# Values product by one level of Strassen, in blocks of 256 queries, with x streamed from memory

## The chip, the cores and the metric

The kernel runs on one NeuronCore of a Trainium2 chip. The metric is the device time of one execution in microseconds (us). The engines are TensorE (PE in profile rows; PEld is its weight load), VectorE (DVE), ScalarE (ACT), GpSimd (POOL) and SyncE (SP), which here issues nearly all DMAs.

## The reference

x is 4096x512, adj is 4096x4096, both float32. Layer 0 is dense attention with adj added twice to the logits; layer 1 is a graph attention of 8 heads.

```python
q, k, v = x @ Wq.T + bq, x @ Wk.T + bk, x @ Wv.T + bv
attn = softmax(q @ k.T / sqrt(512) + adj + adj)
x = layernorm(x + attn @ v)
feats = einsum('nf,hfd->hnd', x, W)
dense = leaky_relu(e_self[:, :, None] + e_neigh[:, None, :]) + NEG_INF * (1.0 - adj)
out = relu(einsum('hnm,hmd->hnd', softmax(dense), feats) + b)
x = layernorm(x + out)
```

With adj up to 5.4 and NEG_INF = -1e10, the second softmax picks one neighbour per row: the one with the largest adj. The kernel finds that column, proves that the pick is safe, and gathers its row of feats; a general path for other inputs stands in the program and is not taken.

## The kernel before, in words

Every float32 matrix is split into two float16 parts, hi and lo, and a product is three matmuls (hi*hi, hi*lo, lo*hi) per 128x128 weight tile (`split_product`, L476). ScalarE makes the hi part, VectorE or GpSimd the lo part.

First stage, over 8 groups of 512 tokens: x is split into `xT`, which stays in SBUF; TensorE makes the values (4 tiles, PSUM banks S) and the transformed queries (4 tiles, banks O); both are split and stored to memory (`v_scratch`, `y_scratch`).

Main loop: 8 blocks of 512 queries by 32 key tiles of 128, 256 steps s. In step s TensorE makes the scores of chunk s: keys on partitions, 12 matmuls of 512 columns (L476, S). VectorE adds adj (`add`, L859) into a slot of `ring` and keeps a running maximum (`maximum`, L871). A block's softmax needs the maximum over all keys, so everything else follows 34 steps later (LAG). For chunk e = s-33 VectorE subtracts the broadcast maximum (`subtract`, L853), ScalarE takes exp into `pf` (L704) and makes the hi part (L653), GpSimd makes the lo part (L430) and adds to the row sums (`sacc`, L438). For chunk s-34 TensorE runs the values product: 4 banks O (128 queries each) by 3 matmuls of 512 columns (`values`, L533).

Once per block (`turn`) VectorE evicts the four banks (`evict`, L896); over the next steps each 128-row tile goes through statistics, normalisation (L912), its split (L768), 8 transposes (L572) and its feats product (12 matmuls, L476 X). Between them VectorE scans adj in 256 pieces of 128x512 with MAX8 (L829) and FIND_INDEX8 (L831). After the last values product come the last block's tiles, 32 indirect gathers of feats on GpSimd, the last layernorm and the output.

Order on each engine is program order; semaphores are counters on which an engine, or SP before a DMA, waits. The S banks alternate, so the scores of chunk c wait for `add` of c-2. The values product waits for the lo part.

## Time and profile before

| | |
|---|---|
| median of 3 runs | 1746.85 us (1746.17 to 1750.89) |
| profiled execution | 1754.84 us |
| its span, first to last instruction | 1753.1 us |
| mean granted TensorE clock | 0.971 |
| scores begin / first values product / last values product ends | 205.6 / 304.2 / 1652.7 us |
| TensorE busy, 490 to 1400 us | 908.75 of 910 us |
| VectorE, GpSimd busy there | 747.40 and 443.02 us |

An engine's busy time counts its instructions; a matmul's end is modelled and overlaps the next start, so for TensorE the spacing of starts is the better measure. "Idle before" is the time an engine sat waiting, with what released it.

### The profile page before, as it was taken

To read this page: it belongs to the slowest core of one execution; us is meant where nothing else is said; L and a number is where in the kernel's file an instruction comes from. 1 tells how busy PE (TensorE), PEld (TensorE's weight loads), DVE (VectorE), ACT (ScalarE), POOL (GpSimd) and SP (SyncE) were. 2 spreads that over 40 slices of the span, in tenths; PEclk is the share of its full clock that TensorE was granted. 3 is DMA by queue.
4 is the path that set the end of the run, shared out by engine and by line. 5 is a ranking of instruction groups with operands and counts; after the bars stand their busy time and mean duration, and the time that the engine had idled before them with its cause. 6 is when DMAs were issued, how large, how long until landed. Compare 5 with 4: busy or idle time off the path is not lost.

```text
span 1753.1 us, 22063 instructions
## 1 busy us (share of the span) xinstructions
PE 1641.7 (94%) x7748; PEld 750.8 (43%) x7748; DVE 1227.6 (70%) x2191; ACT 495.9 (28%) x765; POOL 736.6 (42%) x667
## 2 busy tenths in 40 slices
PE   8989999999999999999999999999999999999830
PEld 3334344444444444444444444444444444444310
DVE  4343255778897879778978797888887888754146
ACT  5334200222232223222222222222222222234327
POOL 2000000546444635464446444543455444568643
PEclk9999999999999999999999999999999999999965
DMA  6443434455555554555555455545555555446348
GB/s 216 145 162 120 166 110 127 151 187 162 180 163 200 172 175 162 181 191 165 166 197 181 162 187 181 186 160 182 168 199 164 173 163 191 139 126 210 109 132 294
DMA packets 150480, 298.25 MB, mean 170 GB/s; under 512 B 16352, under 2 KB 16352, under 8 KB 147424
## 3 DMA queue, kind: packets, MB, share of 16 engines
q1 hardware_dynamic: 147808, 288.42, 50.0%
q0 software_dynamic: 2560, 8.39, 1.5%
q8 instruction: 63, 1.03, 0.2%
q14 instruction: 49, 0.40, 0.1%
HBM read 253.76 MB, written 42.99 MB: 169 GB/s over the span
## 4 chain that ended last, share of the span: by engine, by line
PE 82%; DVE 7%; POOL 4%; ACT 3%; issue 2%; DMA 1%; ACTq 0%; DVEq 0%; SPq 0%; POOLq 0%
PE S L476 39%; PE O L533 32%; PE O L476 5%; PE X L476 4%; POOL ring L458 1%; POOL sacc L438 1%; POOL ring L430 1%; PE X L572 1%; DVE xT L768 1%; PE O L483 1%; DVE xr L896 1%; DVE ring L853 1%; DVE cidx L831 1%; DVE cand L829 1%; ACT xT L653 1%
## 5 line engine op out<-in xcount | busy, mean ns | idle before, releaser
L533 PE MATMUL O<-vring,ring 128*128 128x512 f16 x3072 | 704.6, 380 | 3.1 <-POOL ring L430 3.0
L476 PE MATMUL S<-yb,xT 128*128 128x512 f16 x3072 | 702.4, 380 | 4.2 <-DVE ring L859 4.2
L430 POOL TENSOR_TENSOR ring<-pf,ring 128x512 f16<-128x512 f32 x256 | 296.2, 1157 | 905.3 <-ACT ring L653 905.3
L476 PEld LDWEIGHTS S<-yb,xT 128*128 128x128 f16 x3072 | 301.2, 98 | 371.3 <-issue 7.6
L533 PEld LDWEIGHTS O<-vring,ring 128*128 128x128 f16 x3072 | 299.6, 98 | 358.0 <-issue 7.7
L704 ACT ACTIVATE pf<-ring 128x512 f32<-128x512 f32 x256 | 161.2, 630 | 995.5 <-DVE ring L853 970.0
L438 POOL TENSOR_TENSOR sacc<-sacc,pf 128x512 f32<-128x512 f32 x248 | 330.7, 1334 | 0.0
L859 DVE TENSOR_TENSOR ring<-S,ring 128x512 f32<-128x512 f32 x256 | 176.0, 687 | 176.5 <-PE S L476 169.4
L871 DVE TENSOR_TENSOR mx<-mx,ring 128x512 f32<-128x512 f32 x248 | 215.4, 868 | 8.5
L829 DVE MAX8 cand<-piece 128x8 f32<-128x512 f32 x256 | 175.0, 684 | 27.5 <-DMA piece<-in_adj 26.5
L853 DVE TENSOR_TENSOR ring<-BC,ring 128x512 f32<-128x512 f32 x256 | 172.4, 680 | 10.4 <-PE BC L559 10.4
L831 DVE FIND_INDEX8 cidx<-cand,piece 128x8 uint32<-128x512 f32 x256 | 175.4, 685 | 0.0
L653 ACT ACTIVATE ring<-pf 128x512 f16<-128x512 f32 x256 | 161.2, 630 | 8.1
L476 PE MATMUL S<-ring,xT 128*128 128x512 f16 x384 | 91.1, 398 | 12.3 <-DVE vring L768 12.3
L476 PE MATMUL X<-yb,x1T 128*128 128x512 f16 x384 | 93.5, 396 | 4.5 <-ACT x1T L653 4.5
L476 PE MATMUL O<-xT,ring 128*128 128x512 f16 x384 | 84.2, 379 | 0.0
L806 DVE TENSOR_TENSOR yb<-pf,yb 128x512 f16<-128x512 f32 x32 | 23.2, 725 | 61.8 <-ACT yb L688 61.8
L476 PEld LDWEIGHTS S<-ring,xT 128*128 128x128 f16 x384 | 38.4, 102 | 63.4 <-DVE vring L768 15.2
L476 PEld LDWEIGHTS X<-yb,x1T 128*128 128x128 f16 x384 | 38.5, 101 | 53.7 <-issue 7.2
L476 PEld LDWEIGHTS O<-xT,ring 128*128 128x128 f16 x384 | 37.6, 98 | 45.3
L768 DVE SCALAR_TENSOR_TENSOR vring<-S,vring 128x512 f16<-128x512 f32 x32 | 21.5, 688 | 49.9 <-ACT vring L653 49.9
L443 POOL TENSOR_TENSOR xr<-xr,bvb 128x512 f32<-128x512 f32 x32 | 45.6, 1424 | 0.0
(98 smaller groups left out, 696.8 us busy)
## 6 DMA issues: line engine op xcount, KB each, us to landing
ring<-in_adjT SPq DMA_DIRECT2D x256, 256.0 KB, 3.1
vring<-v_scratch SPq DMA_DIRECT2D x256, 256.0 KB, 2.7
piece<-in_adj SPq DMA_DIRECT2D x256, 256.0 KB, 3.7
ring<-in_xT SPq DMA_DIRECT2D x8, 1024.0 KB, 7.4
v_scratch<-vring SPq DMA_DIRECT2D x32, 256.0 KB, 2.1
y_scratch<-yb SPq DMA_DIRECT2D x8, 1024.0 KB, 4.9
yb<-y_scratch SPq DMA_DIRECT2D x8, 1024.0 KB, 6.7
xr<-in_x SPq DMA_DIRECT2D x32, 256.0 KB, 5.0
```

The lines of the kernel that those rows point to most:

```text
L430: pool.tensor_tensor(ring16[:, e % SLOTS, 1, :], pf[:, e % NPF, :], ring16[:, e % SLOTS, 0, :], ALU.subtract).then_inc(lo_done, 1)
L438: pool.tensor_tensor(sacc[:, :], sacc[:, :], pf[:, e % NPF, :], ALU.add).then_inc(sum_done, 1)
L443: pool.tensor_tensor(xr[:, j, :], xr[:, j, :], bvb[:, :], ALU.add).then_inc(xr_set, 1)
L476: mm = pe.matmul(psum, sta(a, k), mov(b, k), start=(k + a + b == 0), stop=(k == n - 1 and a == 1))
L533: mm = pe.matmul(O[j][:, :], ring16[:, e % SLOTS, a, j * P:(j + 1) * P], vring[:, e % NV, m, :], start=(k + a + m == 0), stop=(k == NT - 1 ...
L653: return nc.scalar.activation(dst, src, ACT.Copy, scale=scale)
L704: nc.scalar.activation(pf[:, e % NPF, :], ring[:, e % SLOTS, :], ACT.Exp, scale=-2.0).then_inc(exp_done, 1)
L829: dve.max(cand[:, q, :], part).then_inc(cand_set, 1)
L831: dve.max_index(cidx[:, q, :], cand[:, q, :], part).then_inc(cidx_set, 1)
L853: dve.tensor_tensor(slot, BC[:, :], slot, ALU.subtract).then_inc(sub_done, 1)
L859: dve.tensor_tensor(slot, S[c % 2][:, :], slot, ALU.add).then_inc(add_done, 1)
L871: dve.tensor_tensor(mx[:, :], mx[:, :], slot, ALU.max).then_inc(max_done, 1)
```

## The change

The values product of a step is now 256 queries (two tiles of 128) by 256 keys (two tiles) by 512 value columns (two halves), seen as a 2x2 by 2x2 product of 128x128 and 128x256 blocks, and done with 7 products instead of 8. Each is three matmuls of 256 columns, so a step has 21 of them where 12 of 512 columns (as much as 24 of 256) stood. The seven stationary operands are sums and differences of exp tiles, made in every step in `pfc`: the sums by GpSimd, the differences by VectorE (`exp_differences`). The seven moving operands are sums and differences of value tiles, made once in the first stage; six stay in SBUF (`vc`), the seventh is streamed (`vsum`). Banks O hold seven accumulators (`PRODUCTS`), and `combine` puts them together once per block, with three copies by ScalarE.

Blocks have 256 queries: 16 blocks of 16 steps, each step 256 keys; the lag is 19 steps. The scores of a step are 24 matmuls of 256 columns. SBUF no longer holds x: its split tiles are streamed through `xring`, five slots of 256 KB, two per chunk, and the weights of the feats product pass through the same slots. GpSimd no longer adds the bias of the values to x (it is in the values). At a turn the scores of two chunks run ahead of the first values product of the next block, and the next step has none. In the last 16 chunks VectorE makes the large lo part (`last_lo`, line 1087) instead of GpSimd. The scan does MAX8 alone; per row tile one piece is gathered again (GpSimd, indirect) and FIND_INDEX8 runs on it (`find`).

```diff
+    QB = 256
+    JB = QB // P
...
+    NP = NT // 2
+    NC = NB * NP
+    G = 512
+    GT = G // P
+    NG = N // G
+    LAG = NP + 3
+    AHEAD = 3
+    SLOTS = LAG + 2
+    NX = 5
+    NVS = 3
     PW = 512
     NPC = N // PW
     NSC = 3
-    STEPS = NC + LAG
-    W1_STEPS = 2
-    assert D == 512 and N % QB == 0 and H * DH == D and NT == 32 and NB == 8
+    FIND_AFTER = 4
+    EG = 4
+    NE = NT // EG
+    assert D == 512 and N == 4096 and H * DH == D
...
+        def scores_at(s):
+            if block_at(s, 0) is not None:
+                chunks = (s, s + 1)
+            elif block_at(s, 1) is not None:
+                chunks = ()
+            else:
+                chunks = (s,)
+            return [c for c in chunks if c < NC]
...
+        def lo_by_vector(e):
+            return e >= NC - NP
...
+                _, (kind, n, part) = stream[i]
+                if i >= NX:
+                    _, (old, m, old_part) = stream[i - NX]
+                    if old == "w":
+                        sp.wait_ge(f_part, m * KC + old_part + 1)
+                    elif old_part == 0:
+                        sp.wait_ge(s_half, m + 1)
+                    else:
+                        sp.wait_ge(s_done, m + 1)
+                src = x_d[2 * (n % NP) + part] if kind == "x" else w1_d[part]
+                sp.dma_start(xring[:, i % NX, :], src).then_inc(x_in[i % NX], 16)
...
-                    pool.tensor_tensor(prod[k][:, kc, :], w1f[:, kc, :], ab[k], ALU.mult).then_inc(prod_set, 1)
...
+            def value_sums(t):
+                if t >= 1:
+                    pool.wait_ge(v_lo, t)
+                pool.wait_ge(vf_set, 2 * t + 2)
+                pair = vf[:, t % 2]
+                flat = pair.rearrange("p k n -> p (k n)")
+                pool.tensor_tensor(vsum32[:, 0:2 * DHALF].rearrange("p (k n) -> p k n", k=2), pair[:, :, 0:DHALF],
+                                   pair[:, :, DHALF:D], ALU.add).then_inc(vsum_set, 1)
+                pool.tensor_tensor(vsum32[:, 2 * DHALF:4 * DHALF], pair[:, 1, :], pair[:, 0, :], ALU.subtract
+                                   ).then_inc(vsum_set, 1)
+                pool.tensor_tensor(vsum32[:, 4 * DHALF:5 * DHALF], flat[:, 0:DHALF], flat[:, 3 * DHALF:4 * DHALF], ALU.add
+                                   ).then_inc(vsum_set, 1)
...
+                    pool.wait_ge(exp_done, e + 1)
+                    pool.tensor_tensor(buf[:, 512:768], buf[:, 0:256], buf[:, 256:512], ALU.add).then_inc(sums_set, 1)
+                    pool.tensor_tensor(buf[:, 1024:1152], buf[:, 0:128], buf[:, 384:512], ALU.add).then_inc(sums_set, 1)
+                    pool.wait_ge(sums_set, 2 * e + 1)
...
+                        pool.tensor_tensor(total, total, buf[:, 512:768], ALU.add).then_inc(sum_done, 1)
+                    pool.wait_ge(hi_done, 2 * e + 1)
+                    pool.tensor_tensor(parts[:, 1, 0:P], buf[:, 0:P], parts[:, 0, 0:P], ALU.subtract).then_inc(lo_first, 1)
+                    if not lo_by_vector(e):
...
+                        pool.tensor_tensor(parts[:, 1, P:7 * P], buf[:, 3 * P:9 * P], parts[:, 0, P:7 * P], ALU.subtract
+                                           ).then_inc(lo_rest, 1)
...
+                for half, done in enumerate((s_half, s_done)):
+                    i = place["x", c, half]
+                    tile = xring[:, i % NX, :].rearrange("p (a c n) -> p a c n", a=2, c=KC)
+                    pe.wait_ge(x_in[i % NX], (i // NX + 1) * 16)
+                    split_product(S[c % 2][:, half * QB:(half + 1) * QB], lambda a, kc: tile[:, a, kc, :],
+                                  lambda m, kc: yb[:, b % 2, m, kc, :], KC).then_inc(done, 1)
...
+            PRODUCTS = ((0, 1, 1, 4), (0, 0, 6, None), (1, 1, 0, 5), (1, 0, 3, 0), (2, 1, 4, 2), (2, 0, 2, 1), (3, 0, 5, 3))
+            FREED = (1, 4, 6, 5)
...
+                pe.wait_ge(vs_in[e % NVS], (e // NVS + 1) * 16)
+                pe.wait_ge(lo_first, e + 1)
+                pe.wait_ge(lo_rest, e + 1)
+                for bank, half, sta, val in PRODUCTS:
+                    opens, closes = half == 1 or bank == 3, half == 0
+                    if opens and k == 0 and b >= 1:
...
                     for a, m in ((0, 0), (0, 1), (1, 0)):
-                        mm = pe.matmul(O[j][:, :], ring16[:, e % SLOTS, a, j * P:(j + 1) * P], vring[:, e % NV, m, :],
-                                       start=(k + a + m == 0), stop=(k == NT - 1 and a == 1))
...
+                        start = opens and k + a + m == 0
+                        dst = O[bank][:, half * DHALF:(half + 1) * DHALF]
+                        mov = vsum[:, e % NVS, m, :] if val is None else vc[:, k, m, val, :]
+                        if start and bank < 3:
+                            dst = O[bank][:, :].rearrange("p (h n) -> p h n", h=2)
+                            mov = zero_then[:, 0:val + 2:val + 1, :]
+                        mm = pe.matmul(dst, pc[:, e % 2, a, sta * P:(sta + 1) * P], mov, start=start,
...
+            for g in range(NG):
+                value_hi(2 * g)
...
+                    act.wait_ge(c_set, 2)
+                query_hi(g, 0)
+                value_hi(2 * g + 1)
+                for jc in range(1, KC):
+                    query_hi(g, jc)
+                if g + 2 < NG:
                     x_hi(g + 2)
                 if g == 1:
...
+                    if e >= 2:
+                        act.wait_ge(pv_done, e - 1)
+                    act.wait_ge(exp_done, e + 1)
+                    buf = pfc[:, e % 2, :]
+                    scaled(pc[:, e % 2, 0, 0:P], buf[:, 0:P], 1.0).then_inc(hi_done, 1)
+                    act.wait_ge(sums_set, 2 * e + 2)
+                    act.wait_ge(diff_set, e + 1)
+                    scaled(pc[:, e % 2, 0, P:7 * P], buf[:, 3 * P:9 * P], 1.0).then_inc(hi_done, 1)
...
+                    if e >= 2:
+                        act.wait_ge(lo_first, e - 1)
+                        act.wait_ge(lo_rest, e - 1)
+                        act.wait_ge(sum_done, e - 1)
+                    nc.scalar.activation(pfc[:, e % 2, 0:512], ring[:, e % SLOTS, :], ACT.Exp, scale=-2.0
...
-                    act.wait_ge(exp_done, e + 1)
-                    scaled(ring16[:, e % SLOTS, 0, :], pf[:, e % NPF, :], 1.0).then_inc(hi_done, 1)
...
+            def value_rows(kt):
+                dve.wait_ge(vp_ready, kt + 1)
+                dve.scalar_tensor_tensor(out=vf[:, kt // 2 % 2, kt % 2, :], in0=S[kt % 2][:, :],
+                                         scalar=V_UP / (W_UP * XT_UP), in1=bvb, op0=ALU.mult, op1=ALU.add
+                                         ).then_inc(vf_set, 1)
...
-                    dve.wait_ge(v_hi, kt + 1)
-                    lo_part(vring[:, kt % NV, 1, :], S[kt % 2][:, :], V_UP / (W_UP * XT_UP), vring[:, kt % NV, 0, :]
-                            ).then_inc(v_lo, 1)
...
-                wait_apart(cand_set, p + 1)
-                dve.max_index(cidx[:, q, :], cand[:, q, :], part).then_inc(cidx_set, 1)
+                dve.max(cand[:, q, :], piece[:, p % NSC, :]).then_inc(cand_set, 1)
...
+            def find(t):
+                wait_apart(won_in, (t + 1) * 16)
+                dve.max_index(wonidx[:, :], top8[:, t % 2, :], won[:, :]).then_inc(wonidx_set, 1)
...
+                dve.tensor_tensor(buf[:, 768:1024].rearrange("p (k n) -> p k n", k=2), quarters[:, :, 1, :],
+                                  quarters[:, :, 0, :], ALU.subtract).then_inc(diff_set, 1)
...
+            def last_lo(e):
...
+                dve.wait_ge(hi_done, 2 * e + 2)
+                dve.tensor_tensor(parts[:, 1, P:7 * P], buf[:, 3 * P:9 * P], parts[:, 0, P:7 * P], ALU.subtract
+                                  ).then_inc(lo_rest, 1)
...
+                dve.tensor_tensor(left, second(0), left, ALU.add).then_inc(c_added, 1)
+                dve.wait_ge(c_copied, 3 * b + 3)
+                dve.tensor_tensor(right, right, second(1), ALU.subtract).then_inc(c_added, 1)
+                dve.wait_ge(c_added, done + 1)
...
+                dve.tensor_tensor(cb[:, 0, 0:DHALF], cb[:, 0, 0:DHALF], O[3][:, 0:DHALF], ALU.subtract).then_inc(c_added, 1)
+                dve.wait_ge(c_added, done + 4)
+                dve.tensor_tensor(cb[:, 1, DHALF:D], O[2][:, DHALF:D], cb[:, 1, DHALF:D], ALU.add).then_inc(c_added, 1)
...
-                    if j < JB - 1:
-                        dve.wait_ge(o_done, b * (JB - 1) + j + 1)
-                    else:
-                        dve.wait_ge(pv_done, (b + 1) * NT)
-                    dve.scalar_tensor_tensor(out=xr[:, j, :], in0=O[j][:, :], scalar=rinv[:, j:j + 1], in1=xr[:, j, :],
-                                             op0=ALU.mult, op1=ALU.add).then_inc(h_set, 1)
+                    dve.wait_ge(c_added, done + 5 + j)
+                    dve.wait_ge(xr_in[j], (b + 1) * 16)
+                    dve.scalar_tensor_tensor(out=xr[:, j, :], in0=cb[:, j, :], scalar=rinv[:, j:j + 1], in1=xr[:, j, :],
+                                             op0=ALU.mult, op1=ALU.add).then_inc(c_added, 1)
```

TensorE at a turn. Before: the last values product of a block with the row sums (L544) in its middle, between two scores.

```order
L476 MATMUL S<-yb,xT 128x512 x12
L533 MATMUL O<-vring,ring 128x512 x6
L544 MATMUL X<-vup,sacc 128x1 x4
L533 MATMUL O<-vring,ring 128x512 x6
L476 MATMUL S<-yb,xT 128x512 x12
```

TensorE now, from the two chunks of scores at a turn: `pc` holds the split exp combinations, `big` the value combinations, `vsum` the streamed one.

```order
L607 MATMUL S<-yb,xring 128x256 x48
L684 MATMUL O<-big,pc 128x512
L684 MATMUL O<-big,pc 128x256 x2
L684 MATMUL O<-vsum,pc 128x256 x3
L684 MATMUL O<-big,pc 128x512
L684 MATMUL O<-big,pc 128x256 x5
L684 MATMUL O<-big,pc 128x512
L684 MATMUL O<-big,pc 128x256 x11
L684 MATMUL O<-vsum,pc 128x256 x3
L684 MATMUL O<-big,pc 128x256 x15
L607 MATMUL S<-yb,xring 128x256 x24
```

Scores and values are now all of 256 columns, but for three matmuls of 512 that open a block's banks; two values products follow each other after the double scores.

GpSimd in the main loop before: one step, and the two small operations (L449, L451) of one row tile's normalisation.

```order
L430 TENSOR_TENSOR ring<-pf,ring 128x512
L438 TENSOR_TENSOR sacc<-sacc,pf 128x512
L449 TENSOR_TENSOR ve<-mv,eps 128x1
L451 TENSOR_TENSOR rstd<-ve,mhalf 128x1
L430 TENSOR_TENSOR ring<-pf,ring 128x512
```

GpSimd now, one step of the main loop: two sums of exp quarters, the row sums, the lo part of the first tile and of the other six; then, once per row tile of the scan, the gather.

```order
L556 TENSOR_TENSOR pfc<-pfc 128x256
L557 TENSOR_TENSOR pfc<-pfc 128x128
L565 TENSOR_TENSOR sacc<-sacc,pfc 128x256
L567 TENSOR_TENSOR pc<-pfc,pc 128x128
L570 TENSOR_TENSOR pc<-pfc,pc 128x768
L544 DMA won<-in_adj,wonrow 128x512
```

Five operations per step stand where two stood, 1536 elements a partition where 1024 stood; L443, the bias, is gone.

VectorE at a turn, before: `evict` between two steps' work.

```order
L871 TENSOR_TENSOR mx<-mx,ring 128x512
L888 RECIPROCAL rinv<-X 128x4
L896 SCALAR_TENSOR_TENSOR xr<-O,rinv,xr 128x512 x4
L853 TENSOR_TENSOR ring<-BC,ring 128x512
L829 MAX cand<-piece 128x8
L831 MAX_INDEX cidx<-cand,piece 128x8
```

VectorE now, at the last turn before the end, when the scores are done: `combine` and one step (L1079 is the difference, L1087 the lo part by VectorE).

```order
L1135 RECIPROCAL rinv<-X 128x2
L1138 TENSOR_TENSOR hc<-O,hc 128x2x256
L1140 TENSOR_TENSOR hc<-hc,O 128x2x256
L1142 TENSOR_TENSOR hc<-hc,O 128x256
L1144 TENSOR_TENSOR hc<-hc,O 128x256
L1147 TENSOR_TENSOR hc<-hc,O 128x256
L1149 TENSOR_TENSOR hc<-O,hc 128x256
L1154 SCALAR_TENSOR_TENSOR hc<-hc,rinv 128x512 x2
L1079 TENSOR_TENSOR pfc<-pfc 128x256
L1094 TENSOR_TENSOR big<-BC,big 128x512
L1087 TENSOR_TENSOR pc<-pfc,pc 128x768
```

Eight operations after the reciprocal stand for four, and two operations with both inputs in SBUF stand in the step.

## Rows read from the trace of the kernel before

**Rows 1.** The profile's page: busy time, share of the span, instructions of each engine.

```profile
PE 1641.7 (94%) x7748; PEld 750.8 (43%) x7748; DVE 1227.6 (70%) x2191; ACT 495.9 (28%) x765; POOL 736.6 (42%) x667
```

**Rows 2.** Busy time by window: microseconds, engines, clock, DMA share, GB/s.

```profile
490.00:1400.00 910.00, 908.75 (x4354) 420.31 (x4354) 747.40 (x1333) 236.93 (x365) 443.02 (x386) 1.00 0.55 178
```

**Rows 3.** Timeline of TensorE in the steady stretch: start, duration, operation.

```profile
799.62 2.75 PE L476 MATMUL S<-yb,xT 128*128 128x512 f16 x12
802.21 2.75 PE L533 MATMUL O<-vring,ring 128*128 128x512 f16 x12
```

**Rows 4.** Timeline of TensorE: small matmuls, each with its own weight load.

```profile
19.77 0.94 PE L491 MATMUL X<-bq,ring 128*128 128x2 f16 x32
...
1561.31 0.62 PE L572 MATMUL X<-ident,x1h 128*128 128x128 f16 x8 [0.29 <-DVE x1h L768]
1561.77 0.60 PE L533 MATMUL O<-vring,ring 128*128 128x512 f16 x2
```

**Rows 5.** Groups by line: busy, mean ns of one, idle before and releaser.

```profile
L438 POOL TENSOR_TENSOR sacc<-sacc,pf 128x512 f32<-128x512 f32 x248 | 330.7, 1334 | 0.0
L476 PEld LDWEIGHTS S<-yb,xT 128*128 128x128 f16 x3072 | 301.2, 98 | 371.3 <-issue 7.6 <-DVE ring L859 4.6
...
L430 POOL TENSOR_TENSOR ring<-pf,ring 128x512 f16<-128x512 f32 x256 | 296.2, 1157 | 905.3 <-ACT ring L653 905.3
L871 DVE TENSOR_TENSOR mx<-mx,ring 128x512 f32<-128x512 f32 x248 | 215.4, 868 | 8.5
...
L831 DVE FIND_INDEX8 cidx<-cand,piece 128x8 uint32<-128x512 f32 x256 | 175.4, 685 | 0.0
...
L853 DVE TENSOR_TENSOR ring<-BC,ring 128x512 f32<-128x512 f32 x256 | 172.4, 680 | 10.4 <-PE BC L559 10.4
L653 ACT ACTIVATE ring<-pf 128x512 f16<-128x512 f32 x256 | 161.2, 630 | 8.1
```

**Rows 6.** One line at a time: duration min/median/max, and a 64-element DVE operation.

```profile
L871 DVE TENSOR_TENSOR mx<-mx,ring x248: 691/693/1761, 216.1 to 1540.0; 128x512 f32<-128x512 f32 x124
...
L449 POOL TENSOR_TENSOR ve<-mv,eps x32: 186/636/646, 481.7 to 1673.9; 128x1 f32<-128x1 f32 x32
...
L653 ACT ACTIVATE ring<-ring x6: 1056/1057/1911, 4.1 to 66.2; 128x1024 f16<-128x1024 f32 x4, 128x2048 f16<-128x2048 f32 x2
...
910.43 0.25 DVE L839 TENSOR_TENSOR gidx<-cidx,offs 128x64 f32<-128x64 uint32 x1
```

**Rows 7.** Timeline of GpSimd and VectorE around one running maximum.

```profile
802.91 1.27 POOL L438 TENSOR_TENSOR sacc<-sacc,pf 128x512 f32<-128x512 f32 x1
803.21 1.52 DVE L871 TENSOR_TENSOR mx<-mx,ring 128x512 f32<-128x512 f32 x1
```

**Rows 8.** Timeline of TensorE and VectorE in the first stage.

```profile
44.59 2.29 DVE L768 SCALAR_TENSOR_TENSOR xT<-ring,xT 128x2048 f16<-128x2048 f32 x1 [1.10 <-ACT xT L653]
...
47.54 5.35 PE L476 MATMUL S<-ring,xT 128*128 128x512 f16 x24 [0.90 <-DVE vring L768]
...
71.54 8.17 PE L476 MATMUL S<-ring,xT 128*128 128x512 f16 x24 [3.11 <-DVE vring L768]
```

**Rows 9.** Timeline where the scores begin: TensorE and the DMA queue.

```profile
205.55 5.34 PE L476 MATMUL S<-yb,xT 128*128 128x512 f16 x24
207.76 0.32 SPq L281 DMA_DIRECT2D y_scratch<-yb  x1
208.56 2.16 SPq L293 DMA_DIRECT2D ring<-in_adjT  x3
...
215.05 83.21 PE L476 MATMUL S<-yb,xT 128*128 128x512 f16 x372 [4.16 <-DVE ring L859]
```

**Rows 10.** DMA issues: KB each, median microseconds from issue to landing.

```profile
ring<-in_adjT SPq DMA_DIRECT2D x256, 256.0 KB, 3.1
vring<-v_scratch SPq DMA_DIRECT2D x256, 256.0 KB, 2.7
```

**Rows 11.** Timeline of TensorE after the last values product.

```profile
1651.22 1.46 PE L533 MATMUL O<-vring,ring 128*128 128x512 f16 x6
...
1667.74 4.45 PE L476 MATMUL X<-yb,x1T 128*128 128x512 f16 x12 [1.12 <-ACT x1T L653]
...
1681.79 2.76 PE L476 MATMUL X<-yb,x1T 128*128 128x512 f16 x12 [1.12 <-ACT x1T L653]
```

784 lines of the change are left out of this document (456 added, 328 removed).

## The prediction

> **What bounds the kernel now.** I read the page first: TensorE is busy 94% of the span, VectorE 70%, GpSimd 42% [rows 1]. Then the busy time by window: from 490 to 1400 us TensorE is busy 908.75 of 910 us at clock 1.00, so only TensorE's own work counts there; VectorE is at 747/910 = 82%, GpSimd at 49%, the DMA engines at 0.55 [rows 2]. The timeline gives the unit: twelve matmuls of 512 columns start 2.59 us before the next twelve, 215.8 ns each, so a step costs 5.18 us [rows 3]. At 2.4 GHz 512 columns are 213.3 ns, so each matmul has 2.5 ns on top and its weight load is hidden. Outside that stretch the timeline shows three losses: TensorE waiting for VectorE in the first stage [rows 8], for adj when the scores begin [rows 9], and the serial row tiles after the last values product [rows 11].
>
> **What TensorE's work becomes.** No 256-column matmul stands in the trace. I take 106.7 + 2.5 = 109.2 ns. The bounds: below, half of 215.8, 107.9. Above, eight transposes of 128 columns, each with its own weight load, take 0.46 us to the next start, 57.5 ns where 53.3 + 2.5 = 55.8 would be expected: 1.7 ns more. And 32 matmuls of 2 columns with 32 loads take 0.94 us, at most 29 ns a pair, so a load can be fed every 29 ns although its row says 98 ns [rows 4, 5]. I take 109.2 because the load fits three times behind it; the other end, 110.9, costs 1.7 x 45 x 256 = +20 us.
> - Scores: 24 x 109.2 = 2.62 us for 2.59, x256: +7.9.
> - Values: 21 x 109.2 = 2.29 for 2.59, x256: -76.0.
> - The 512-column openings: 3 per block x 16 x 0.107: +5.1.
> - Row sums, maxima and broadcast 16 times instead of 8, about 1.6 us each where 2.5 stood: +6.
> - In the loop lie 30 row tiles instead of 28, each a feats product of 2.59 and transposes of 0.46 [rows 3, 4]: +6.1; the tail's side of this comes below.
> Sum: -51, from 1431 us between 205.6 us and the end of the values (256 x 5.18, 28 x 3.05, 8 x 2.5) to 1380. A step is 4.91 us; with feats and the rest of the block spread over 16 steps, 5.4.
>
> The Trainium skill, "TensorE: Matmul & The Clock Gate", section "Back-to-back issue gap", says that in a stream of load and matmul pairs a 128-column matmul costs about 81 ns where one alone costs 56, since the load takes part of the time. Were these 25 ns added to each of 45 matmuls a step, the sum would be 288 us higher. The transposes' 57.5 ns speak against it.
>
> **What the other engines must do in 4.91 us.** GpSimd: 512 elements to float16 take 1.157 us, a float32 sum 1.27 undisturbed (the group's mean of 1334 ns holds disturbed ones), one element at least 0.186 [rows 5, 6, 7]. So some 2.1 ns an element and, back to back, 0.15 us apiece: 0.69 + 0.42 + 0.69 + 0.39 + 1.59 = 3.77 us for 2.4 before. VectorE and GpSimd exclude each other: a running maximum that starts 0.30 us into a GpSimd sum ends 0.55 us after it and takes 1.52 us instead of 0.69, while the median of all 248 is 693 ns [rows 6, 7]. The subtraction, which reads PSUM, stays at 680 ns [rows 5]. So the two can only take turns: 3.77 + 0.55 (maximum) + 0.28 (the new difference, 256 elements; 0.25 us for 64 and 0.69 for 512 give 0.44 in all) = 4.60 us. With a block's other such work (two last steps of combine, two normalisations and splits, 3.1 us, and GpSimd's four small operations, 2.5, an estimate from the 0.64 us of L449) and the gathers (1.2 us per 7.3 steps) it is 5.1 of 5.4. VectorE in all: 0.68 + 0.68 + 0.69 + 0.44, MAX8 1.1 x 0.68, 2.1 us per row tile of the scan, 11.4 us per block: 4.2 us a step, for which 175 + 24 us of FIND_INDEX8 fall away, and 0.8 for being blocked: 5.0 of 5.4. ScalarE has 0.31 + 0.84 (between 630 ns for 512 and 1057 for 1024 elements) + 0.63 = 1.8 us [rows 5, 6]. All fit, with little room, and TensorE waits for the lo part only two steps after its exp. In the full steps I add nothing beyond what is lost today.
>
> **Terms beside that.**
> - First stage: +12. The banks S are freed by `value_rows`, behind `x_lo` on VectorE, as the lo parts are now: x_lo ends at 46.9 and TensorE waited 0.90 us; where it waited 3.11, 24 matmuls then took 8.17 us instead of 5.2, as part of them ran at the lower clock level [rows 8]. The chain now passes GpSimd twice per group (1.22 + 1.22 + 0.69 = 3.1 us), then ScalarE (1.95), VectorE (2.2), three pairs of 1.2 and x_hi, x_lo (1.9, 2.5): it ends some 1.7 us later, in six groups 10 us, and the slow clock costs 0 to 3 us in some of them. Ends: 5 and 25.
> - Scores begin: +5.6. Today two chunks are made before adj lands, and TensorE resumes at 215.05, 9.5 us after it began, 4.3 idle [rows 9]. Now no chunk can start: the first x tile is issued behind the y store and three adj loads (2.2 us) and lands 2.7 later, some 9.8 us after the last query product, and no work is done by then. Ends: 3 and 9.
> - While only scores run: +5. A chunk of 2.62 us needs 768 KB. At 178 GB/s for a share of 0.55 a 2 KB packet takes 101 ns [rows 2]; adj comes in 1 KB packets, which cost 50 to 101. So 2.4 to 3.2 us of each DMA engine per chunk, over 18 chunks: 0 to 11. In full steps it is 3.7 to 4.9 us of 5.4.
> - The weights of feats: +6. Their fourth tile takes the slot that the first half of the same step's scores frees, 1.31 + 3 x 0.65 = 3.25 us before its use, while loads land after 2.7 to 3.1 us [rows 10], later under more load. 0 to 1 us, 30 times; I take 0.2.
> - The last 19 steps, values alone: +26. TensorE would need 2.29 us, 49.6 with two feats. But a round is now exp 0.63, GpSimd's sum 0.69, the difference 0.28, the second sum 0.42, the hi part 0.84 and about 0.35 of signals = 3.2 us, since the next exp stands behind the hi part on ScalarE; 16 rounds 51.2, two steps with GpSimd's lo part at 4.6, the block's work on VectorE (combine, statistics, two tiles, the proof) 13, the last product 2.3: 76. Ends: +12 if the block's work hides, +40. Today these steps lose little, as GpSimd's 2.4 us is under 2.59. Of the 1447.1 us up to 1652.7, 1431 are work, 4.3 the wait for adj and 2.9 the slow clock after it (83.2 us for 31 chunks [rows 9]); 8.8 are other waits, of which I leave 5: -3.8.
> - After the last values product: -12.4. It ends at 1652.7; from one row tile's feats to that two tiles on are 14.05 us, 7.0 a tile at the lower clock level, and two tiles fall away [rows 11]; combine and the weight tiles give back 1.7. The 32 gathers and the last layernorm don't change.
>
> Sum: -51 + 12 + 5.6 + 5 + 6 + 26 - 3.8 - 12.4 = -12.6. Against the profiled execution (span 1753.1, 1754.84 in all, 8 above the median of 1746.85) that is 1742; against the median, rounded, **1735 us**. What a measurement tells from no change is 0.3%, 5.2 us.
>
> **The rivals.**
> - The gain arrives nearly whole, 0.2. The last steps lose 12 (-14), the first stage 5 (-7), the streams 3 (-8): -12.6 - 29, about 1705. For it: exp for two steps ahead, and the lo part of the last block moved off GpSimd. Against it: the round of 3.2 us is in program order.
> - Port bound, slower, 0.22. GpSimd and VectorE take turns through more than the 5.4 us a step; from there each 0.1 us costs 24 us. If GpSimd's five operations take 15% more than my line through two points, 4.33 us, the sum is 5.7: +0.27 x 237 = +64, about 1799; at half of that 1767. For it: 5.1 of 5.4 by my own figures, and VectorE at 5.0. Against: TensorE has run beside 82% on VectorE without loss.
> - DMA bound, 0.1. 1 KB packets at the price of 2 KB ones, and streams that wait for each other in SP's one queue: 4.9 us per step and weights beside. +6 while only scores run, +24 in feats (1 us instead of 0.2), some 6 in turns: +36, 1770. Against: 0.55 today with loads landing in 3 us.
> - Weight loads exposed, 0.03. The load's row is 98 ns, the matmul 109, so 11 ns are left: if the 98 were not hidden at all, 98 x 45 x 256 = +1129 us, 2864. The skill's page would make it 288, about 2022.
> - The forecast, 0.45: own range 1718 to 1755.
>
> **How the numbers follow.** Of the forecast's 0.45, 0.3 lie below 1741.6, 0.12 within 0.3%, 0.03 above; with the first rival 0.2 faster and a little of the DMA case within: faster 0.5, same 0.14, slower 0.36. The range takes the first rival down to 1700 and the port case up to 1795, about two in ten outside.
>
> **What would show it.** Scores groups of 24 in 2.62 us and values of 21 in 2.29; the first values product at about 285 us; waits of TensorE for `vf_set` in the first stage; in the last 19 steps some 4 us between values products, released by VectorE L1087. Steps of over 4.91 us between turns, with GpSimd without a gap, would prove the port case; waits of TensorE for x tiles the DMA case.

## The result and the profile after

The changed kernel takes 1775.12 us in the median of 4 runs (1772.02 to 1778.22), the kernel before beside it 1748.57 (1746.17 to 1750.89): ratio 1.0145, 95% interval 1.0117 to 1.0173. It is some 26 us slower where I forecast 12 us faster. The profiled execution has a span of 1776.3 us (1778.22 in all), 23.2 above that of before; the working below is made against this pair.

The page of the changed kernel, first the busy time, which answers to [rows 1], then SyncE's DMA queue (packets, MB, share of 16 engines):

```profile
PE 1600.0 (90%) x13172; PEld 1283.5 (72%) x13172; DVE 1352.9 (76%) x2241; ACT 621.6 (35%) x1085; POOL 1245.2 (70%) x1461
...
q1 hardware_dynamic: 276560, 419.01, 73.3%
```

TensorE is busy 90% instead of 94%, though it has less to do; GpSimd went from 42% to 70%. The queue moves 419 MB; in the kernel before it was 288 MB and a share of 50.0%.

Windows of the changed kernel (columns as in [rows 2]): the first stage, the stretch with scores alone, and 200 us of full steps.

```profile
core 0: us, PE busy (x) PEld busy (x) DVE busy (x) ACT busy (x) POOL busy (x), PEclk, DMA share, GB/s
50.00:224.50 174.50, 152.46 (x648) 65.83 (x648) 87.98 (x123) 69.03 (x102) 53.85 (x46) 0.90 0.37 129
224.50:283.50 59.00, 47.58 (x410) 41.24 (x410) 24.39 (x38) 1.94 (x4) 0.00 (x0) 0.88 0.84 270
500.00:700.00 200.00, 195.77 (x1732) 167.52 (x1731) 166.12 (x272) 68.03 (x123) 165.80 (x195) 1.00 0.86 275
```

From 500 to 700 us TensorE is busy 195.77 of 200 where it was busy without a gap before [rows 2], the DMA engines at 0.86. The first stage has a mean clock of 0.90: part of it ran at the lower of the two clock levels (1.2 and 2.4 GHz), behind waits of TensorE, as the group shown below.

The timeline of TensorE where the full steps begin, the counterpart of [rows 3]:

```profile
296.57 2.78 PE L607 MATMUL S<-yb,xring 128*128 128x256 f16 x24
299.19 0.49 PE L684 MATMUL O<-big,pc 128*128 128x256 f16 x3
...
299.84 1.80 PE L684 MATMUL O<-big,pc 128*128 128x256 f16 x15
301.48 2.78 PE L607 MATMUL S<-yb,xring 128*128 128x256 f16 x24
```

24 score matmuls from 296.57 to 299.19, 2.62 us; 21 of values to 301.48, 2.29 us; a step of 4.91. These are the figures of the forecast to the hundredth, so what it says of TensorE's own work stands, and the cause must lie outside it. It lies mostly in the waits. TensorE's waits over the whole kernel (us in total, times, longest):

```profile
PE S L607 <- DVE big L979: 25.9, 7, 6.7
PE X L735 <- DMA xring<-w_scratch: 20.4, 19, 2.4
PE X L724 <- DVE x1h L963: 14.7, 7, 7.3
PE S L607 <- DMA xring<-x_scratch: 11.4, 1, 11.4
PE X L724 <- DVE hc L1179: 10.9, 10, 1.6
...
PE O L684 <- DMA vsum<-vsum_scratch: 5.8, 2, 4.5
```

None of these is a wait for GpSimd (the whole list has one, 1.0 us, in the last steps), or for x tiles in full steps. Each is at a seam or at a row tile's work: the value rows of the first stage (L979), the weight tiles of feats, the split of x1 in the last steps and the tail (L963), the first x tile, the eviction of one row tile's feats before the next one's transposes (L1179).

With the milestones of the two timelines the whole difference can be laid out against the terms of the forecast:

| term | forecast | measured | how it is read |
|---|---|---|---|
| TensorE's work | -51 | -51 | unit prices above; the two traces' own counts at these prices give some -53 |
| first stage | +12 | +19 | last query product ends at 224.65, before at 205.7 |
| scores begin | +5.6 | +7.1 | 11.4 idle; before 4.3 lost |
| scores alone | +5 | 0 | 17 chunks in 47.42, 2.9 over 17 x 2.62, as much as before [rows 9] |
| weight tiles | +6 | +20.4 | 19 waits |
| last 19 steps | +26 | +27 | 84.1 from the last scores' start, less 2.6 of scores and 54.4 of TensorE's work |
| other waits to the end of the values | -3.8 | +10.6 | what is left of +33.1 (1652.7 to 1685.85); 10.1 of L1179, before 2.4 for the same eviction (L921) |
| after the last values product | -12.4 | -9.9 | 90.4 us, before 100.4; the stores of the result span 37.6 and 37.3 us, so the pair is alike there |
| sum | -12.6 | +23.2 | |

Two places show how the larger terms came about. First stage, one group of the changed kernel, all engines:

```profile
93.74 1.27 POOL L523 TENSOR_TENSOR pfc<-big 128x512 f32<-128x512 f32 x1 [7.18 <-DVE vsum L963]
...
97.40 0.63 ACT L808 ACTIVATE big<-big 128x512 f16<-128x512 f32 x1 [2.64 <-POOL pfc L527]
...
99.31 0.69 DVE L963 SCALAR_TENSOR_TENSOR big<-big 128x512 f16<-128x512 f32 x1 [3.75 <-ACT vsum L808]
...
105.27 2.50 DVE L963 SCALAR_TENSOR_TENSOR xring<-big,xring 128x512 f16<-128x512 f32 x4 [1.11 <-ACT xring L808]
107.68 2.28 DVE L1036 TENSOR_REDUCE u<-big 128x32 f32<-128x2048 f32 x1
...
109.88 1.28 DVE L979 SCALAR_TENSOR_TENSOR big<-S,big 128x512 f32<-128x512 f32 x2
```
```profile
110.61 7.86 PE L607 MATMUL S<-big,hc 128*128 128x512 f16 x24 [4.21 <-DVE big L979]
```

VectorE waits 3.75 us for the chain value sums (GpSimd) and float16 parts (ScalarE), so its lo part begins at 99.31; behind it stand the queries' lo parts and `x_lo` of the group after next, 105.27 to 107.7, and in this group a reduction. Only then come the value rows that free the banks S: TensorE waits 4.21 us and then takes 7.86 us for 24 matmuls, more than the 5.2 that they take at full clock.

The weight tiles: TensorE, and SyncE's queue with the same tile.

```profile
394.53 2.10 PE L735 MATMUL X<-xring,x1T 128*128 128x512 f16 x9
397.62 0.82 PE L735 MATMUL X<-xring,x1T 128*128 128x512 f16 x3 [0.99 <-DMA xring<-w_scratch]
```
```profile
393.41 0.74 SPq L372 DMA_DIRECT2D xring<-w_scratch  x1
394.72 2.26 SPq L372 DMA_DIRECT2D xring<-x_scratch  x4
```

The last weight tile is issued at 393.41, right after the slot's half of the scores (begun at 391.91) is read, and TensorE is ready for it at 396.6. It is let go at 397.62: 4.2 us from issue, where the forecast had 3.25 us of room against loads of 2.7 to 3.1 [rows 10]. It is the same in the others: 15 of the 19 tiles that TensorE waited for were issued within 0.07 us of the end of the matmuls that freed their slot, and the 19 landed 3.3 to 5.4 us after their issue. Under the new traffic the median of these loads is 3.9 us, in full steps 4.3.

### The profile page after: what moved, and what is told of

The parts are those of the page before. It is cut to its first block, busy times and chain, and to the rows that moved or that the text cites. A ratio compares the mean times of both kernels' runs of the same rounds, so it can differ in the third digit from the quotient of the medians.

```text
span 1776.3 us, 36165 instructions
## 1 busy us (share of the span) xinstructions
PE 1600.0 (90%) x13172; PEld 1283.5 (72%) x13172; DVE 1352.9 (76%) x2241; ACT 621.6 (35%) x1085; POOL 1245.2 (70%) x1461
## 4 chain that ended last, share of the span: by engine, by line
PE 64%; DVE 11%; POOL 8%; DMA 7%; issue 5%; ACT 4%; SPq 1%; ACTq 0%; DVEq 0%; POOLq 0%
PE S L607 32%; PE O L684 26%; DMA xring<-w_scratch 5%; PE X L735 3%; DVE big L963 2%; POOL big L589 1%; POOL pfc L556 1%; POOL pc L570 1%; DMA vsum<-vsum_scratch 1%; PE X L724 1%; DVE pfc L1079 1%; POOL pfc L557 1%; POOL pfc L525 1%; DVE cand L1052 1%; DVE big L1101 1%
## 5 line engine op out<-in xcount | busy, mean ns | idle before, releaser
L607 PE MATMUL S<-yb,xring 128*128 128x256 f16 x6144 | 710.2, 273 | 11.4 <-DMA xring<-x_scratch 11.4
L607 PEld LDWEIGHTS S<-yb,xring 128*128 128x128 f16 x6144 | 602.5, 98 | 84.9 <-issue 11.9
L684 PE MATMUL O<-big,pc 128*128 128x256 f16 (+1 forms) x4608 | 599.8, 276 | 11.8 <-DMA vsum<-vsum_scratch 5.8
L808 ACT ACTIVATE pc<-pfc 128x128 f16<-128x128 f32 (+1 forms) x512 | 289.1, 574 | 862.1 <-PE O L684 549.0
L684 PEld LDWEIGHTS O<-big,pc 128*128 128x128 f16 x4608 | 453.2, 99 | 80.8 <-issue 7.8
L570 POOL TENSOR_TENSOR pc<-pfc,pc 128x768 f16<-128x768 f32 x240 | 396.0, 1650 | 137.1 <-ACT pc L808 136.1
L1101 DVE TENSOR_TENSOR big<-S,big 128x512 f32<-128x512 f32 x256 | 175.6, 686 | 177.5 <-PE S L607 177.0
L556 POOL TENSOR_TENSOR pfc<-pfc 128x256 f32<-128x256 f32 x256 | 233.1, 911 | 79.8 <-ACT pfc L901 79.1
L1113 DVE TENSOR_TENSOR mx<-mx,big 128x512 f32<-128x512 f32 x240 | 238.6, 994 | 8.2
L565 POOL TENSOR_TENSOR sacc<-sacc,pfc 128x256 f32<-128x256 f32 x240 | 212.6, 886 | 0.0
L1079 DVE TENSOR_TENSOR pfc<-pfc 128x256 f32<-128x256 f32 x256 | 186.4, 728 | 0.1
L735 PE MATMUL X<-xring,x1T 128*128 128x512 f16 x384 | 96.5, 394 | 23.0 <-DMA xring<-w_scratch 20.4
```

The lines of the kernel that those rows point to most:

```text
L556: pool.tensor_tensor(buf[:, 512:768], buf[:, 0:256], buf[:, 256:512], ALU.add).then_inc(sums_set, 1)
L565: pool.tensor_tensor(total, total, buf[:, 512:768], ALU.add).then_inc(sum_done, 1)
L570: pool.tensor_tensor(parts[:, 1, P:7 * P], buf[:, 3 * P:9 * P], parts[:, 0, P:7 * P], ALU.subtract).then_inc(lo_rest, 1)
L607: mm = pe.matmul(psum, sta(a, k), mov(b, k), start=(k + a + b == 0), stop=(k == n - 1 and a == 1))
L684: mm = pe.matmul(dst, pc[:, e % 2, a, sta * P:(sta + 1) * P], mov, start=start, stop=(k == NP - 1 and a == 1 and closes))
L735: mm = pe.matmul(X[:, :], x1T[:, a, kc, :], weights[:, m, :], start=(kc + a + m == 0), stop=(kc == KC - 1 and a == 1))
```

## The experiments

Ratios are against the kernel before, run beside it on the same chip; the changed kernel has 1.0145. Differences in us are against the changed kernel: difference of the ratios times 1749. The ratio of the changed kernel is itself known to 0.0028, 5 us, and that stands in every difference. "The stretch" is the time from the start of the last scores to the end of the last values product.

### Feats after the values product (e1)

```diff
@@ TensorE, one step @@
+                if 0 <= s - LAG < NC:
+                    values(s - LAG)
                 for j in range(JB):
...
                         feats(b * JB + j)
-                if 0 <= s - LAG < NC:
-                    values(s - LAG)
@@ VectorE: ahead of add(s); SyncE's store of feats the same @@
-                    b = block_at(s, 4 + 2 * j)
+                    b = block_at(s, 5 + 2 * j)
                     if b is not None:
                         evict_feats(b * JB + j)
```

> Edit: within a step TensorE does the transposes of x1 and the feats product after the values product instead of before it (2.29 us later); the store of feats and its eviction move one step on. Theory A (a latency of the transfer, hidden by 2.3 us): the waits for weight tiles (20.4 us in 19 of them, longest 2.4) fall to under 3 us, those for the eviction L1179 (10.9 us) to under 4; no new wait; time 24 us under the changed kernel, about 1751. Rival B (the queue is short of bandwidth, so the wait only moves): TensorE waits for x tiles or vsum instead, gain under 8 us, 1767 or more.

Measured: 1766.18 us, ratio 1.0047 (1.0025 to 1.0069), 17 us less, between the two. TensorE's waits in it:

```profile
PE X L724 <- DVE hc L1179: 15.6, 11, 3.0
PE S L607 <- DMA xring<-x_scratch: 13.9, 6, 11.4
...
PE X L735 <- DMA xring<-w_scratch: 0.8, 1, 0.8
```

The waits for weight tiles fall from 20.4 us to 0.8: theory A. A shift of 2.29 us, with the traffic unchanged, removes them, so it is a latency and not a lack of bandwidth; of x tiles 2.5 us of waits are new, besides the first of 11.4. My second expectation missed: the waits for the eviction L1179 grew from 10.9 to 15.6, as on VectorE it now stands behind the scan (ahead of the scan, in e9, they are 6.0). That is part of why 17 and not 24 us came; the waits for L1087 grew too, from 3.5 to 8.2, and those for GpSimd's lo part from 1.0 to 3.1.

### The first x tiles ahead of the last query store (e2)

```diff
@@ SyncE, first stage, last group @@
+                if g == NG - 1:
+                    for c in range(AHEAD):
+                        load_adj(c)
...
+                    for i in range(NX):
+                        load_passing(i)
                 sp.wait_ge(y_lo, (g + 1) * KC)
```

> Edit: the first three adj loads and the first five x tiles are issued before the store of the last query block instead of behind it. Theory A: the 11.4 us in which TensorE waits for the first x tile after the last query product go, but for 1 to 2 us of VectorE's last value rows: 10 us less than the changed kernel, about 1765. Rival B: the loads now collide with the stores of the first stage and the wait turns into one for adj or y: gain under 4 us.

Measured: 1779.27 us, ratio 1.0124 (1.0095 to 1.0153), 4 us less with an interval that includes no change. SyncE's queue shows why the wait for the first x tile only fell from 11.4 to 7.8 us:

```profile
217.70 8.13 SPq L378 DMA_DIRECT2D vsum_scratch<-vsum  x2
...
227.47 2.54 SPq L350 DMA_DIRECT2D xring<-x_scratch  x5
```

The store of the last value sums stands ahead of the moved loads, and it waits for VectorE until 225.5. So neither theory as written: the edit came too late in the queue. In the combined kernels below the loads stand ahead of these stores as well, x tiles first, and there the gap is 0.5 us.

### x_lo one group later (e3)

```diff
@@ VectorE, first stage @@
                 for i in range(GT):
                     value_rows(g * GT + i)
+                    if i == 1 and 1 <= g < NG - 1:
+                        x_lo(g + 1)
...
-                if g + 2 < NG:
-                    x_lo(g + 2)
```

> Edit: VectorE splits x for group g+1 (x_lo) after the second value row tile of group g instead of at the end of group g-1. Theory A (VectorE's order: x_lo's 2.5 us stand ahead of the value rows that free the banks S): the 25.9 us of waits for L979 fall to 8 or less and part of the slow clock behind them goes; last query product ends at 206 to 212 instead of 224.5 us; time 15 us less, about 1760. Rival B (the chain through GpSimd's three sums is itself too long): the waits stay above 18 us, gain under 5 us.

Measured: 1761.44 us, ratio 1.0026 (1.001 to 1.0041), 21 us less: theory A, beyond its figure, though the waits did not fall to 8. The last query product ends at 203.5 us instead of 224.65.

```profile
192.96 10.52 PE L607 MATMUL O<-hc,big 128*128 128x512 f16 x48
```
```profile
PE S L607 <- DVE big L979: 13.1, 5, 7.2
```

25.9 us of waits fall to 13.1, and the mean clock of the first stage from 50 us on rises from 0.90 to 0.98, which is the rest of the 21. GpSimd's sums, which I had made the cause of the +12, are all still there, and so are half of the waits; the next run bears on what they are worth.

### The same edit in the kernel before (e12)

```diff
@@ VectorE of the kernel before, first stage @@
                             ).then_inc(v_lo, 1)
+                    if kt == g * JB + 1 and 1 <= g < NB - 1:
+                        x_lo(g + 1)
...
-                if g + 2 < NB:
-                    x_lo(g + 2)
```

> The kernel before, with the one edit of e3_xlo_next: VectorE splits x for group g+1 after the second value tile of group g. It asks how much of that edit belongs to the change. Theory A (the old order cost the kernel before its 12.3 us of waits for the lo parts of the values, and slow clock behind two of them): most of it goes, 8 to 13 us less, ratio 0.993 to 0.995. Rival B (most of the 12.3 us comes from elsewhere in VectorE's order): under 4 us less. In the changed kernel the same edit gave about 21 us.

Measured: 1735.22 us, ratio 0.9923 (0.9902 to 0.9944), 14 us less than the kernel before: theory A, a little beyond its range. The order cost the kernel before too: its waits for the lo parts of the values fall from 12.3 to 2.7 us, and its last query product ends at 188.8 us instead of 205.7.

```profile
178.24 10.52 PE L476 MATMUL O<-xT,ring 128*128 128x512 f16 x48
```

So of the 21 us some 14 are no matter of the change. What the old order costs the changed kernel beyond that is 7 us by the ratios, with as much uncertainty, and 4 by the ends of the last query product (21.2 us sooner there, 17.0 here). But with the new order in both kernels the changed one still ends its query products 14.7 us later (203.5 against 188.8), with 13.1 us of waits where 2.7 are left: most of the first stage's +19 is the change's own and does not hang on this order.

### Three more matmuls in every step (e4)

```diff
@@ TensorE, values @@
-                    for a, m in ((0, 0), (0, 1), (1, 0)):
+                    passes = ((0, 0), (0, 1), (1, 0)) * (2 if bank == 3 else 1)
+                    for i, (a, m) in enumerate(passes):
```

> Edit: the last of the seven products is done twice in every step, 24 matmuls instead of 21, so that one product counts double in the output. Theory A (TensorE paces the full steps): 3 x 109.2 ns x 256 = 84 us more than the changed kernel, less what the last steps hide (16 x 0.33 = 5): 1851 to 1860. Rival B (GpSimd, VectorE or the DMA queue pace the steps): part of it is hidden, under 60 us more, 1835 or less.

Measured: 1844.68 us, ratio 1.0494 (1.0465 to 1.0523), 61 us more, between the two and at the edge of B (1835 us on the scale of 1749). The steps themselves follow A:

```profile
707.20 0.49 PE L685 MATMUL O<-big,pc 128*128 128x256 f16 x3
...
707.86 2.13 PE L685 MATMUL O<-big,pc 128*128 128x256 f16 x18
709.82 2.78 PE L607 MATMUL S<-yb,xring 128*128 128x256 f16 x24
712.44 0.49 PE L685 MATMUL O<-big,pc 128*128 128x256 f16 x3
```

from one values product to the next 5.24 us, 4.91 + 0.33. But a block of 16 steps grows by 3.8 us (88.2 to 92.0, the mean of the 15 intervals between the transposes of row maxima in TensorE's timeline) and not by 5.2. Part of what is missing is found in shorter waits: weight tiles 20.4 to 16.1, L1179 10.9 to 3.6. Waits that are a fixed delay from an earlier event shrink when TensorE comes later to them. I read it so that a matmul saved in such a step is worth about three quarters of its time; that the shorter waits are all of the difference isn't shown.

### One more sum on GpSimd in every step (e7)

```diff
@@ GpSimd, at the end of a step @@
+                    pool.tensor_tensor(extra[:, 0:256], b1b[:, 0:256], b1b[:, 256:512], ALU.add)
```

> Edit: GpSimd does one more float32 sum of 256 elements in every step, into a scratch tile that nobody reads (0.69 us undisturbed, about 0.9 with what VectorE keeps from it). GpSimd is busy some 4.5 us of 5.57 a step now. Theory A (there is room in GpSimd between turns, but little): TensorE still takes 4.91 us between turns, and only the turns lose: 10 to 40 us more. Rival B (GpSimd and VectorE together already pace the kernel): 0.7 to 0.9 us a step, 140 to 200 us more. Rival C (much room): under 5 us.

Measured: 1813.18 us, ratio 1.0349 (1.0321 to 1.0377), 36 us more: theory A, near its upper end. Windows and TensorE's timeline of this kernel:

```profile
500.00:700.00 200.00, 190.59 (x1682) 161.97 (x1680) 171.33 (x265) 67.01 (x120) 187.58 (x225) 1.00 0.85 269
```
```profile
704.28 0.49 PE L686 MATMUL O<-big,pc 128*128 128x256 f16 x3
...
709.19 0.49 PE L686 MATMUL O<-big,pc 128*128 128x256 f16 x3
```

GpSimd is busy 187.58 of 200 us, 94%, and between turns TensorE still goes at 4.91 us. The 36 us come in the steps with a block's work, where waits for x1 grow from 14.7 to 29.5 us, those for the row maxima from 2.1 to 6.5 and those for GpSimd's lo part from 1.0 to 8.0. So the rival of the port, whose sign was to be steps of over 4.91 us between turns, shows itself in the block's work first, and the changed kernel has stayed below it: 165.80 of 200 us.

### The x1 loads in small pieces (e5)

```diff
@@ SyncE @@
             def load_x1(e):
-                first, last = 2 * e * EG, min(2 * (e + 1) * EG, NT - JB)
+                first, last = 2 * e, 2 * e + 2
...
-                e, r = divmod(s - (NC - NP + 6 + LAG), 5)
-                if r == 0 and 0 <= e < NE // 2:
+                e = s - (NC - NP + 2 + LAG)
+                if 0 <= e < NT // 2 - 1:
```

> Edit: the last-layernorm loads of x1, four of eight row tiles that stand among the loads of the last steps in SyncE's queue, are split into fifteen of two row tiles, one per step. Theory A (a vsum load stands behind 2 MB of x1 in the queue): the two waits for vsum (5.8 us together, the long one 4.5) go and the slow clock behind them; from the last scores to the last values product 84.1 us become 76 to 79; time 6 us less than the changed kernel. Rival B (the end is paced by the exp round of VectorE, ScalarE and GpSimd, and the wait only covers it): the stretch stays above 82, gain under 3 us.

Measured: 1768.26 us, ratio 1.0114 (1.0088 to 1.0139), 5 us less with an interval that includes no change; but the stretch is 78.5 us instead of 84.1: theory A, by the trace. (The small loads also begin four steps sooner.) What it removes is seen in the changed kernel, SyncE's queue and then TensorE:

```profile
1654.99 0.38 SPq L404 DMA_DIRECT2D big<-x_scratch  x1
1656.37 2.70 SPq L389 DMA_DIRECT2D vsum<-vsum_scratch  x2
1659.17 0.96 SPq L444 DMA_DIRECT2D hc<-in_x  x2
```
```profile
1666.28 0.82 PE L684 MATMUL O<-big,pc 128*128 128x256 f16 x3 [4.50 <-DMA vsum<-vsum_scratch]
```

2 MB of x1 are issued at 1654.99, ahead of the value sums, and TensorE waits 4.50 us for the latter.

### The last steps: exp first, and the lo part back on GpSimd (e6, e11)

```diff
@@ ScalarE, one step @@
+                pair = (exp_of, hi_of) if lo_by_vector(s - LAG + 1) else (hi_of, exp_of)
+                for part in pair:
+                    part(s)
```

`hi_of` and `exp_of` hold what stood here in this order, the float16 parts and the next exp.

> Edit: in the last 16 chunks ScalarE computes the next exp before the large float16 part of the current chunk, not after it. The round in the changed kernel is 3.06 us in the steps with no other work (exp, two sums, the difference, the float16 part, one behind the other). Theory A: it becomes float16 part, VectorE's lo part, exp: 0.84 + 0.97 + 0.61 and some 0.3 of signals = 2.7 us, 16 x 0.35 = 5 us less where it paces, so 3 to 6 us less than the changed kernel. Rival B: the work on the block (combine, statistics, x1) and the x1 loads set the length of the stretch (84.1 us): under 2 us gained.

Measured: 1782.19 us, ratio 1.0187 (1.0167 to 1.0207), 7 us more, and the stretch 91.2 us. Both theories fell. One round, VectorE and ScalarE of this kernel:

```profile
1658.19 1.23 DVE L1094 TENSOR_TENSOR pc<-pfc,pc 128x768 f16<-128x768 f32 x1 [1.63 <-ACT pc L808]
1659.34 0.67 DVE L1086 TENSOR_TENSOR pfc<-pfc 128x256 f32<-128x256 f32 x1
1659.94 0.68 DVE L1101 TENSOR_TENSOR big<-BC,big 128x512 f32<-128x512 f32 x1
```
```profile
1660.65 0.63 ACT L889 ACTIVATE pfc<-big 128x512 f32<-128x512 f32 x1 [2.49 <-DVE big L1101]
...
1664.71 0.63 ACT L889 ACTIVATE pfc<-big 128x512 f32<-128x512 f32 x1 [2.50 <-DVE big L1101]
```

Exp now waits 2.5 us for the subtraction (L1101 of that kernel), which in VectorE's order stands behind the lo part and the difference of the chunk before; I had followed ScalarE's dependences and left out VectorE's queue. The round is 4.06 us (1660.65 to 1664.71) instead of 3.06.

```diff
             def lo_by_vector(e):
-                return e >= NC - NP
+                return False
```

> The changed kernel with one edit: in the last 16 chunks GpSimd makes the large lo part as in all others, not VectorE. GpSimd then does all five operations, 4.5 us a step, where the round is 3.06 now. Theory A (in the last steps the chain through GpSimd and VectorE paces, not TensorE's 2.29 us): some 4.5 us a step, the stretch from the last scores to the last values product grows from 84.1 to 98 to 108, 15 to 24 us more than the changed kernel, ratio 1.023 to 1.028. Rival B (block work and loads set the stretch): under 5 us more.

Measured: 1787.77 us, ratio 1.0167 (1.0132 to 1.0202), 4 us more with an interval that includes no change; the stretch is 84.3 us as in the changed kernel: rival B. The round in steps with no other work is longer, 3.95 us, and several steps with block work are shorter; that VectorE has the lo part off its hands there would explain it, but is not shown apart. It also gives GpSimd's five operations back to back:

```profile
1659.29 1.64 POOL L570 TENSOR_TENSOR pc<-pfc,pc 128x768 f16<-128x768 f32 x1
1660.89 0.91 POOL L556 TENSOR_TENSOR pfc<-pfc 128x256 f32<-128x256 f32 x1
...
1662.17 0.72 POOL L565 TENSOR_TENSOR sacc<-sacc,pfc 128x256 f32<-128x256 f32 x1
...
1663.24 1.64 POOL L570 TENSOR_TENSOR pc<-pfc,pc 128x768 f16<-128x768 f32 x1
```
```profile
1659.69 1.52 DVE L1079 TENSOR_TENSOR pfc<-pfc 128x256 f32<-128x256 f32 x1 [1.83 <-ACT pfc L901]
```

3.95 us from one lo part to the next, of which the forecast's 3.77 is 5% short. The difference on VectorE starts inside GpSimd's lo part, at 1659.69, and ends 0.28 us after it, at 1661.21: the two do not run at once, as in [rows 7].

### All together (e8, e9, e10)

The first combined kernel has the edits of e1 (the eviction ahead of the scan), e2 (loads ahead of the last two stores), e3, e5 and e6.

> Edits together: feats after the values product (with its eviction ahead of the scan on VectorE), x_lo one group later, x1 loads in small pieces, exp ahead in the last chunks, and the first x tiles and adj loads issued before the last two value sums are stored. Theory A (the losses are separate waits at the seams, not one resource): the gains add up: 17 + 22 + 10 + 6 + 4 = 59 us under the changed kernel, ratio to the kernel before 0.98. Rival B (the DMA queue, busy 0.8 to 0.86, or GpSimd takes part of it back): 40 us or less, ratio 0.992 or more.

Measured: 1725.21 us against 1750.25 of the kernel before, ratio 0.9852 (0.9828 to 0.9875), 51 us less than the changed kernel, between A and B; its stretch of last steps is 92.5 us, the price of the exp order. Without it:

> All the edits of e8_all but the exp order, which lengthened the last steps (round 4.06 us where 3.06 stood). Expected: from the last scores to the last values product 78 to 80 us instead of 92.5, so 13 us less than e8_all, ratio to the kernel before 0.978 (0.975 to 0.981). If the separate seams did not add up, the stretch would stay over 85.

Measured: 1720.83 us against 1760.31, ratio 0.9775 (0.974 to 0.981), 65 us less than the changed kernel, as expected. Its windows and waits:

```profile
500.00:700.00 200.00, 197.96 (x1765) 171.19 (x1763) 168.12 (x282) 68.77 (x127) 163.38 (x194) 1.00 0.86 273
```
```profile
PE S L607 <- DVE big L979: 13.3, 5, 7.1
PE O L684 <- DVE pc L1087: 8.4, 5, 3.0
```

The last query product ends at 202.9, scores begin at 203.4, the last stretch takes 78.1 us; the DMA engines are as full as in the changed kernel. The single edits gave 17, 4, 21 and 5 us, and the better place for the first loads 7 more (7.8 us of wait to 0.5): 54, and the whole gives 65. The whole is known to some 8 us and the sum to some 20, since the changed kernel's own uncertainty enters it four times; within that the losses add up.

> As e9_four, and VectorE's eight small operations of the proof (3 us, in the last steps ahead of the next difference) stand after the loop, where VectorE waits for the gathers. Theory A (VectorE's block work on the last steps is the chain of exp, difference, float16 part): 3 to 4 us less than e9_four, ratio 0.976. Rival B (something else, the normalisation of x1 or ScalarE, paces those steps): under 1 us less.

Measured: 1720.06 us, ratio 0.9777 (0.9743 to 0.9811), the same as e9: rival B. The stretch is 79.5 us, not shorter.

## Why the prediction was wrong

**Right.** The price of a matmul (109.2 ns), a step of 4.91 us, the place of most losses, and no wait for GpSimd between turns. All but two terms have the right sign. The last steps, +27 for +26, are right partly by luck: 5.8 us of them are waits for value sums behind the x1 loads, which the forecast did not have (e5 takes 5.6 us off the stretch), and the round it priced at 3.2 us is 3.06 where it stands alone. That 1772 (1.0145 x 1746.85) lies inside the range is luck too: it lies there only by the cases of the port and of the DMA. The Trainium skill, "TensorE: Matmul & The Clock Gate", section "Back-to-back issue gap", would have had a 128-column matmul in a stream of loads and matmuls cost 25 ns more; the 24 score matmuls in 2.62 us leave 2.5 ns beside the 106.7 of their columns, so this trace shows none of it for 256 columns.

**The step that failed** is "the weights of feats: +6", with its sentence "I take 0.2" us for each of 30. Measured: 20.4 us in 19 waits, up to 2.4. I took 3.25 us of room against landings of 2.7 to 3.1 us, rows of a kernel whose DMA engines were at 0.55, and only added "later under more load". At 0.86 the median is 4.3 in full steps. A margin of 0.15 us over the longest of those landings, when the traffic grows by half, was no margin; the price of 1 us stood in the text, but in the DMA rival. That rival's number, 1770, came close, but not its form (streams short of bandwidth): with scores alone nothing was lost, 0 for +5, and e1 shows the waits go by a shift.

**The second** is "other waits -3.8". I took over the waits of before as a sum, 5 of 8.8, while a turn now comes every 16 steps of 4.91 us and VectorE is fuller. It came out 14.4 higher, 19.4 where 5 were left. The trace names 13.6 us of such waits before the last steps (7.6 in the kernel before): 10.1 in nine waits for L1179 (2.4 in five before), 2.0 for x1 and 1.5 for the row maxima. TensorE's own work, counts times unit prices, comes to 1375 us and not to 1380, so some 11 us remain, small gaps and stretches just under full clock for which the trace names no releaser (4 before). e7 shows that block work is where pressure on GpSimd and VectorE comes out. What makes up those 11 us stays open.

**The third** is the first stage, +19 for +12. The mechanism, VectorE reaching the value rows late, was right, and in the main the size: with the order of e3 in both kernels the changed one still takes 14.7 us longer. What the term took over without a price is the place of `x_lo`, ahead of the value rows: the old order costs the kernel before 17.0 us and the changed one 21.2, so some 4 of the 19 come from that order and the change together. How much of the 14.7 is the chain through GpSimd that I charged, and how much VectorE's own work, is not shown.

The rest is small: scores begin +1.5, last steps +1, tail +2.5. All but one of the errors have one sign, and they come to 36 us; I had priced each seam near its undisturbed value, and the forecast of -12.6 was smaller than that. The full gain (1705) would have needed seams that cost nothing: e9 reaches 1710 on this scale (0.9775 x 1749) after four edits of order.

**The change itself.** If a product saved is worth what one more costs in e4, seven products for eight gain some 61 us, and the rebuilt kernel spends 87 elsewhere. Put in a better order it is 2.25% faster than the kernel before, and, as the intervals stand (0.9775 against 0.9923), about 1.5% faster than the kernel before with the one edit that helps both.

## What to carry to other kernels

Price every wait against the latency under the new traffic, not the old: here a landing went from 3 to 4.3 us as the DMA engines went from 0.55 to 0.86 busy, and a slot freed 3.25 us before use turned into 20 us. When a change saves work on the engine that paces, look for its cost in the order of instructions at the seams (first stage, turns, last steps, queue order), where each loss is small, of one sign, and cheap to remove. And before a dependence is reordered, follow the queue of every engine on the chain: exp first looked free on ScalarE and cost 1 us a round on VectorE's order.

## What the runs showed of the hardware

In e7 GpSimd at 94% with VectorE at 86% (187.58 and 171.33 of 200 us), of which one waits for the other as in [rows 7], still let TensorE go at 4.91 us a step between turns. The Trainium skill, "SBUF — State Buffer", section "SBUF: two separate sides", says that of a GpSimd operation and a VectorE operation with two SBUF inputs the one that starts first keeps the shared port for its whole instruction. The rows of e11 agree: VectorE's difference, started 1.24 us before the end of GpSimd's lo part, ends 0.28 us after it.

The time from the last values product to the end differs between executions of kernels that are the same there: 90.4 us in the changed kernel and 101.4 in e1. The stores of the result differ, not the gathers: SyncE's rows for them span 37.6 and 48.6 us. The difference goes with the surroundings and not with the kernel: e1 to e4 and e9 to e11 take 97 to 101 us there, and the kernel before took 1758 and 1760 us beside them; e5 to e8 take 87 to 91, and the kernel before took 1750. So ratios are to be compared, not times.
